# Mamba layer: the seven-tap convolution of the projected channels written as seven shifted projections

## The reference

```
zxbcdt = einsum('bld,ed->ble', u, W_in)          # u: normed x, 128 features
z, xBC, dt_raw = split(zxbcdt)                   # 256, 512 and 8 columns
xc = conv(transpose(xBC), conv_w, pad 3 and 3)   # 7 taps, each channel by itself
xBC = silu(transpose(xc + conv_b))               # x (256), and B and C of two directions
dt  = softplus(dt_raw + dt_bias)
...                                              # two scans over the tokens (forward, backward)
y = norm_w * (y / rms) * silu(z);  return y @ W_out
```

## Time and profile before

| | |
|---|---|
| median of 3 runs | 5271.6 us (5269.07 to 5281.68) |
| the profiled execution's own time | 5270.87 us |
| its span, first to last instruction | 5269.1 us |
| TensorE busy | 83% of the span |
| VectorE busy | 62% |
| ScalarE busy | 53% |
| GpSimd busy | 22% |
| mean granted TensorE clock | 0.87 of full |

### The profile page before, as it was taken

How to read it: one execution, slowest core, us unless ns; L and a number is a source line. 1 busy time by engine, 2 the same in 40 slices (tenths; PEclk the granted TensorE clock), 3 DMA queues, 4 the chain that set the end, 5 groups by cost and what they waited for, 6 DMA issues and landing times.

```text
span 5269.1 us, 95794 instructions
## 1 busy us (share of the span) xinstructions
PE 4377.1 (83%) x38234; PEld 1845.2 (35%) x38234; DVE 3290.1 (62%) x4913; ACT 2818.4 (53%) x5188; POOL 1137.6 (22%) x1318
## 2 busy tenths in 40 slices
PE   4888867888876657745699999999999999999995
PEld 2333433434444424423123333333222222333343
DVE  4778434344533564553797777676798999776831
ACT  2667533132222222230386667776789888666761
POOL 2221011011000222222123323242211112232413
PEclk7999988788887666565799999999999999999997
DMA  2222010000000000000211011101011111111000
GB/s 80 54 55 55 2 35 21 2 20 9 13 1 7 0 0 1 0 0 27 49 45 38 14 38 20 38 14 38 14 45 44 44 32 33 38 20 38 14 2 17
DMA packets 100288, 133.85 MB, mean 25 GB/s; under 512 B 48194, under 2 KB 60994, under 8 KB 99348
## 3 DMA queue, kind: packets, MB, share of 16 engines
q1 hardware_dynamic: 99860, 127.92, 9.9%
HBM read 63.50 MB, written 54.00 MB: 22 GB/s over the span
## 4 chain that ended last, share of the span: by engine, by line
PE 41%; DVE 8%; ACT 2%; issue 1%; POOL 1%; DMA 0%; SPq 0%; POOLq 0%; DVEq 0%; ACTq 0%
PE ps L1058 14%; PE ps L1031 8%; PE ps L1088 6%; DVE stream_max_pieces L1236 6%; PE ps L1043 5%; PE ps L1135 5%; PE ps L1077 1%; PE ps L1083 1%; ACT stream_probs L1153 1%; PE ps L1107 0%; PE ps L1120 0%; DVE stream_stats L1292 0%; DVE stream_stats L1273 0%; ACT L1153 0%; SPq L1471 0%
## 5 line engine op out<-in xcount | busy, mean ns | idle before, releaser
L1236 DVE TENSOR_REDUCE stream_max_pieces<-ps 128x2 f32<-128x1024 f32 x1536 | 1808.8, 1216 | 415.7 <-PE ps L1043 410.6
L1153 ACT ACTIVATE stream_probs<-ps 128x512 f32<-128x512 f32 x3072 | 1655.6, 597 | 486.5 <-PE ps L1031 468.0
L1058 PE MATMUL ps<-stream_probs,stream_v 128*16 128x256 f32 x12288 | 986.4, 394 | 20.6 <-issue 19.9
L1043 PE MATMUL ps<-stream_k_stack,stream_q_stack 48*128 48x512 bf16 x3072 | 645.3, 394 | 97.9 <-DVE stream_max_pieces L1236 64.6
L1031 PE MATMUL ps<-stream_q_stack,stream_k_stack 51*128 51x512 bf16 x3072 | 657.2, 394 | 13.7 <-ACT stream_probs L1153 9.3
L683 DVE TENSOR_REDUCE alibi_max_pieces<-ps 128x2 f32<-128x1024 f32 (+3 forms) x384 | 355.4, 952 | 140.6 <-PE ps L528 131.3
L1058 PEld LDWEIGHTS ps<-stream_probs,stream_v 128*16 128x16 f32 x12288 | 202.8, 94 | 654.1 <-issue 431.9
L624 ACT ACTIVATE alibi_probs<-ps 128x512 f32<-128x512 f32 (+3 forms) x768 | 333.9, 492 | 177.5 <-PE ps L509 142.9
L1031 PEld LDWEIGHTS ps<-stream_q_stack,stream_k_stack 51*128 51x128 bf16 x3072 | 173.1, 93 | 724.3 <-ACT stream_probs L1153 581.9
L308 POOL CAST stream_negmax_parts<-stream_negmax_t 128x32 bf16<-128x32 f32 x96 | 20.3, 212 | 1442.0 <-DVE stream_negmax_t L1225 1404.2
L1088 PE MATMUL ps<-stream_x1T,stream_w 128*128 128x512 f32 x512 | 282.6, 642 | 0.0
(11 more groups left out here) (412 smaller groups left out, 5752.0 us busy)
## 6 DMA issues: line engine op xcount, KB each, us to landing
stream_q_terms_dram<-stream_q_parts SPq DMA_DIRECT2D x72, 256.0 KB
stream_k_terms_dram<-stream_k_parts SPq DMA_DIRECT2D x72, 256.0 KB
stream_q_stack<-stream_q_terms_dram SPq DMA_DIRECT2D x96, 192.0 KB, 3.8
stream_k_stack<-stream_k_terms_dram SPq DMA_DIRECT2D x96, 192.0 KB, 4.4
delta_v_shifted<-delta_v_padded SPq DMA_DIRECT2D x64, 158.0 KB, 3.5
alibi_q_terms_dram<-alibi_q_parts SPq DMA_DIRECT2D x24, 256.0 KB
alibi_k_terms_dram<-alibi_k_parts SPq DMA_DIRECT2D x24, 256.0 KB
alibi_q_stack<-alibi_q_terms_dram SPq DMA_DIRECT2D x32, 192.0 KB
```

Source lines behind the costliest of these rows:

```text
L1043: ins = e.matmul(c.ps[:, mbank(key) + r, :], qs[R, buf, pair, qt * P:(qt + 1) * P], ks[R, buf, pair, kh * 512:kh * 512 + 512], start=True, ...
L1058: ins = e.matmul(c.ps[32 * j:32 * j + 16, 7, Q], v[:, b % 2, kt, GH * g + j, :], pr[:, (u + j // 2) % RP, j % 2, Q], start=(n == 0 and k = ...
L1153: e.activation(pr[:, u % RP, r, :], c.ps[:, ebank(key), :], ACT.Exp, scale=SCALE).then_inc(s_ed, 1)
L1236: e.tensor_reduce(mx[:, j % 2, kh, 4 * pair + qt % 4, :], c.ps[:, mbank(key):mbank(key) + 2, :], AXX, ALU.max).then_inc(s_md, 1)
```

## The change

The convolution and the projection are both linear along different axes, so the sum over taps can be taken over projections: for tap j the projection weights are scaled, column by column, by that tap, and are multiplied with `xT` shifted by j tokens; seven such products are accumulated in PSUM. `xT` gets three zero columns at either end, `pre` is gone, and `conv_out` too.

- `conv_rows` is a new input, 128 x 7 x 512 float32, 1792 KB: each row holds all taps of the 512 channels. It is loaded with the layer's weights.
- VectorE makes the scaled weights `wc` (`mamba_shifted_weights`) once, with seven products of 128x512, ahead of its first norm.
- TensorE does 56 matmuls of 512 columns per batch in place of 8.
- ScalarE applies bias and Silu straight from PSUM, in place of the copies into `pre`; the four Silus behind the first exponential are gone.
- VectorE's 28 operations per batch (lines 2475, 2478) are gone.

```diff
@@ -159,13 +159,13 @@
-    def __init__(self, core, name, ctx, banks, eps=1e-5):
-        self.c, self.banks, self.eps = core, banks, eps
+    def __init__(self, core, name, ctx, banks, eps=1e-5, pad=0):
+        self.c, self.banks, self.eps, self.pad = core, banks, eps, pad
         self.stats = core.sb(name + "_stats", [P, TPB, 6], F32, ctx)
...
         self.xn = core.sb(name + "_xn", [P, TPB, D], F32, ctx)
-        self.xT = core.sb(name + "_xT", [P, L], F32, ctx)
+        self.xT = core.sb(name + "_xT", [P, L + 2 * pad], F32, ctx)
         self.s_stats = core.sem(name + "_stats_done")
@@ -211,7 +211,7 @@
         for h in range(2):
-            e.activation(self.xT[:, h * 512:(h + 1) * 512], self.c.ps[:, self.banks[h], :], ACT.Copy).then_inc(self.s_xT, 1)
+            e.activation(self.xT[:, self.pad + h * 512:self.pad + (h + 1) * 512], self.c.ps[:, self.banks[h], :], ACT.Copy).then_inc(self.s_xT, 1)
@@ -2229,12 +2229,15 @@
     core.load(name, tri, "triangles")
+    rows = core.sb("conv_rows", [P, TAPS, 4 * P], F32)
+    core.load(name, rows, "conv_rows")
...
     with ExitStack() as ctx:
-        norm = Norm(core, name, ctx, (0, 1))
+        norm = Norm(core, name, ctx, (0, 1), pad=TAPS // 2)
+        xT = norm.xT[:, TAPS // 2:TAPS // 2 + L]
         sb = lambda n, shape, dt=F32: c.sb(f"{name}_{n}", shape, dt, ctx)
-        pre = sb("preconv", [P, 4, L + TAPS - 1])
+        wc = sb("shifted_weights", [P, TAPS, 4 * P])
         act = sb("conv_out", [P, 3, L])
@@ -2286,20 +2289,22 @@
             e.wait_ge(norm.s_xT, 2 * (b + 1))
-            for i in range(4):
-                if i >= 2:
-                    e.wait_ge(s_pjc, 4 * b + i - 1)
-                for k in range(2):
-                    m = e.matmul(bank(2 + 2 * (i % 2) + k), w[:, MW_X + i * P:MW_X + (i + 1) * P], norm.xT[:, k * 512:(k + 1) * 512], start=True, stop=True)
+            e.wait_ge(s_wc, TAPS)
+            for q, i in enumerate((3, 2, 0, 1)):
+                if q >= 2:
+                    e.wait_ge(s_act, 4 * b + q - 1)
+                for j in range(TAPS):
+                    for k in range(2):
+                        m = e.matmul(bank(2 + 2 * (q % 2) + k), wc[:, j, i * P:(i + 1) * P], norm.xT[:, k * 512 + j:k * 512 + j + 512], start=(j == 0), stop=(j == TAPS - 1))
                 m.then_inc(s_pj, 1)
             for t in range(NC_):
-                m = e.matmul(bank(0, 8 * t, 8), norm.xT[:, t * P:(t + 1) * P], w[:, MW_DT:MW_DT + 8], start=True, stop=True)
+                m = e.matmul(bank(0, 8 * t, 8), xT[:, t * P:(t + 1) * P], w[:, MW_DT:MW_DT + 8], start=True, stop=True)
             m.then_inc(s_dtr, 1)
...
                 for t in range(4):
-                    m = e.matmul(bank(6 + t // 2, (t % 2) * SI, SI), norm.xT[:, (4 * r + t) * P:(4 * r + t + 1) * P], w[:, MW_Z:MW_Z + SI], start=True, stop=True)
+                    m = e.matmul(bank(6 + t // 2, (t % 2) * SI, SI), xT[:, (4 * r + t) * P:(4 * r + t + 1) * P], w[:, MW_Z:MW_Z + SI], start=True, stop=True)
                 m.then_inc(s_z, 1)
@@ -2312,7 +2317,7 @@
                 if n < 2:
-                    e.wait_ge(s_pjc, 4 * b + 4)
+                    e.wait_ge(s_act, 4 * (b + 1))
                 else:
@@ -2391,9 +2396,10 @@
             norm.scalar(e, b)
-            for i in range(4):
-                e.wait_ge(s_pj, 4 * b + i + 1)
-                e.activation(pre[:, i, 3:3 + L], flat(2 + 2 * (i % 2)), ACT.Copy).then_inc(s_pjc, 1)
+            for q, i in enumerate((3, 2, 0, 1)):
+                e.wait_ge(s_pj, 4 * b + q + 1)
+                dst = cs[:, 1:1 + L] if i == 3 else act[:, i, :]
+                e.activation(dst, flat(2 + 2 * (q % 2)), ACT.Silu, bias=w[:, MW_CB + i:MW_CB + i + 1]).then_inc(s_act, 1)
             for r in range(2):
@@ -2408,12 +2414,6 @@
                 e.activation(ex[:, n % 2, :], bank(2 + n % 2), ACT.Exp).then_inc(s_ex, 1)
-                if n == 0:
-                    for q, i in enumerate((3, 2, 0, 1)):
-                        e.wait_ge(s_cv, TAPS * (4 * b + q + 1))
-                        alone(e, c)
-                        dst = cs[:, 1:1 + L] if i == 3 else act[:, i, :]
-                        e.activation(dst, conv_out[:, i, :], ACT.Silu).then_inc(s_act, 1)
             for g in range(6):
@@ -2434,13 +2434,13 @@
-    conv_out = mm[:, 0:8, :, :].rearrange("p (i a) h t -> p i (a h t)", i=4)
...
         e.wait_ge(s_w, n_w)
-        e.memset(pre[:, :, 0:3], 0.0).then_inc(s_pad, 1)
-        e.memset(pre[:, :, L + 3:L + 6], 0.0).then_inc(s_pad, 1)
+        e.memset(norm.xT[:, 0:3], 0.0).then_inc(s_pad, 1)
+        e.memset(norm.xT[:, L + 3:L + 6], 0.0).then_inc(s_pad, 1)
+        for j in range(TAPS):
+            e.tensor_tensor(wc[:, j, :], w[:, MW_X:MW_X + 4 * P], rows[:, j, :], ALU.mult).then_inc(s_wc, 1)
         e.memset(cs[:, 0:1], 0.0).then_inc(s_pad, 1)
@@ -2464,18 +2464,6 @@
-            for q, i in enumerate((3, 2, 0, 1)):
-                e.wait_ge(s_pjc, 4 * b + i + 1)
-                for j in range(TAPS):
-                    tap = w[:, MW_CONV + TAPS * i + j:MW_CONV + TAPS * i + j + 1]
-                    src = pre[:, i, j:j + L]
-                    if j == 0:
-                        alone(e, c)
-                        e.tensor_scalar(conv_out[:, i, :], src, tap, w[:, MW_CB + i:MW_CB + i + 1], ALU.mult, ALU.add).then_inc(s_cv, 1)
-                    else:
-                        e.wait_ge(s_cv, TAPS * (4 * b + q) + j)
-                        e.scalar_tensor_tensor(out=conv_out[:, i, :], in0=src, scalar=tap, in1=conv_out[:, i, :], op0=ALU.mult, op1=ALU.add).then_inc(s_cv, 1)
@@ -2593,6 +2581,8 @@
     cols += [np.broadcast_to(rows, (P, rows.size))]
+    taps = np.concatenate(tiles(conv[0:256], conv[256:512]), 0).T
+    r["conv_rows"] = np.ascontiguousarray(np.broadcast_to(taps[None], (P,) + taps.shape))
     r["w_mamba"] = np.ascontiguousarray(np.concatenate(cols, 1))
```

More of the change, by code:

```diff
@@ L2267, in mamba @@
     s_v, s_ms, s_pe, s_ri, s_yn, s_yT, s_yTc, s_o, s_x = S("vector_steps"), S("squares_summed"), S("eps3_added"), S("rms_inv_ready"), S("y_ready"), S("y_transposed"), S("yT_copied"), S("out_ready"), S("residual_ready")
-    s_zw = S("z_weighted")
+    s_zw, s_wc = S("z_weighted"), S("weights_shifted")
     NVS = 4 + 1
```

4 lines of the change are left out of this document (2 added, 2 removed).

## The result

The changed kernel takes 5285.3 us (median of 15 runs; the kernel before 5265.5 in its 15 runs, 6 us under the median of the three runs shown ahead). The ratio is 1.0042, with a 95% interval of 1.0026 to 1.0059: slower by 14 to 31 us. The prediction said 5301, 5284 to 5320, and +30.4 us.

The account below looks back on a forecast made before the run. The prediction took VectorE's convolution, for which TensorE waits 34.35 us per batch, as the bound. 164.8 - 137.4 - 0.7 - 3.7 + 4.4 + 3.0 = +30.4 us on 5270.9 gave 5301 us, range 5284 to 5320.

Parts of the forecast that it names:

- TensorE's added run: Projection: 96 more records per batch at 0.429 us each, hidden behind nothing, 41.2 us per batch, +164.8 us in all.
- rival of closer spacing: Folded projection: the long run's records lie closer than the short one's; 0.031 us less each takes 14 us; chance 0.02.
- rivals of 0.527: Folded projection: records spaced 0.527 us as in the alternating pairs, +44 us, 5345 us; chance 0.05.
- half clock in the run: Folded projection: TensorE at half clock in the run, 48 us more per batch, +192 us, 5493 us; chance 0.03.
- The wait removed: Decay loop's start: TensorE no longer waits for the convolution's last tile and its Silu, -137.4 us over four batches.
- GpSimd's first products: Ahead of the loop: GpSimd's first two products no longer slowed beside VectorE's convolution in two batches, -0.7 us.
- The clock in the loop: Decay loop's first 20 us: slow stretches 2.0 us shorter per batch, -3.7 us; bounds -15.3 and +0.9.
- Behind the loop: From the transposes to the residual, four batches: no change predicted, 0.
- Start of the layer: Once per run: waiting for 1792 KB more of loads, +4.4 us, and seven weight products ahead of the first norm, +3.0.
- The sum: All terms of the prediction together: +30.4 us on 5270.9, giving 5301 us.
- The rival "the clock does not fall": TensorE keeps full clock through the 4.77 us gap ahead of the sums: -22.8 us, 5279 us; chance 0.07.

Follow-up runs that it names:

- one_tap: The changed kernel with only the middle of the seven taps multiplied, the other six left out of the computation; ratio to the kernel before 0.9747, layer 631.9 us.
- wait_filled_37: The kernel before, with 37 matmuls whose result nobody reads put where TensorE waits for the Silus; ratio to the kernel before 0.9988, layer 753.6 us.
- half_each: The changed kernel with two tiles folded on TensorE, two convolved by VectorE, dt and z ahead of the folded matmuls; ratio to the kernel before 0.9812.
- gap_filled: The changed kernel with five unread matmuls of 512 columns in TensorE's gap ahead of the decay sums; ratio to the kernel before 1.0015, layer 774.8 us.
- bf16_folded: The changed kernel with bf16 operands in the folded products, dt and z left in float32; ratio to the kernel before 0.9753, layer 654.5 us.
- late_products: The changed kernel with conv_rows on its own semaphore and the seven weight products behind VectorE's first norm; timed once, 5281.6 us, layer 782.3 us.
- rates_first: The changed kernel with dt and half of z ahead of the folded matmuls, the rest of z between them; ratio to the kernel before 0.9965, layer 764.4 us.

## Why the prediction was right, and where it was not

**How close it was.** The layer's +24.4 on the base that the prediction used, 5270.9, would be 5295, inside the forecast's own 5288 to 5312. The measured 5285.3 is outside of that and only 1 us above the lower end of the wider 5284 to 5320. By the prediction's mark of 5287.4 for slower, worked out from three runs of the kernel before, 5285.3 alone would not be slower; it is against the 15 runs beside it, and by the layer.

**TensorE's added run** (+164.8): right, +164.6. The three things that the old projection did not show (accumulation, 48 us at a stretch, a new weight at each tap) cost nothing, and the shifted reads neither. The rival of closer spacing falls: 0.43 per record over 112 records, and the 0.213 of bf16 fits a price by the pass. So do the rivals of 0.527 and of half clock in the run.

**The wait removed** (-137.4) and GpSimd's first products (-0.7): right. No wait of L2329 for a Silu is left; sums to first loop product take 0.65 us less over the four batches.

**The clock in the loop** (-3.7): right in sign, wrong in size, and this is the step that failed. I wrote that the clock would rise as long after the loop's start as it did after the resumption. The piece from the sums to the transposes fell by 151.1 us; less 137.4 and 0.7 that leaves -13.0, near the lower bound of -15.3 that the text gave for four stretches as short as 4.4. By the same sum: 42.8 slow us before, 22.8 after, of which 8.0 are first products that were slow before too; 28.0 less x 0.46 = 12.9. one_tap shows that a short run with the same gap brings 46.8 slow us, so the length hangs on more than the loop itself, which my rule left out.

**Behind the loop** (0): +3.4. Windows of the stage from the transposes to the residual, second batch, in the kernel before and in the changed one:

```profile
1988.75:2087.65 98.90, 75.69 (x293) 0.57 0.00 0
```

```profile
2006.90:2107.40 100.50, 77.29 (x293) 0.56 0.00 1
```

Slow for 85 us and then for 88, with the same 293 records. wait_filled_37 has +6.4 in this stage. But a fast loop does not by itself cost it: half_each, whose four loops run at full clock, has 397.1 us here against the 398.1 of the kernel before, gap_filled 399.2 and bf16_folded 406.4. No edit touches the stage, and what sets its clock was not tried.

**Start of the layer** (+4.4 and +3.0): +4.6 and +2.9. late_products took both away, but for 1 us of the products.

**The sum** (+30.4): +24.4 in the layer. The 6.0 us between them are the clock's: 9.3 more gained in the loop, 3.4 lost behind it. The time itself came 16 us under the 5301 of the prediction: 6 of it are this, another 5.4 the base (5270.9 against 5265.5), and the rest, under 5 us, no run explains. That these errors went the same way and still stayed inside the range is luck.

**The rival "the clock does not fall"** (0.07) did not happen: the gap still cost the clock in all four batches. gap_filled shows what it would have been: 774.8 us of layer, +10.5 and not the +7.6 of its price.

**Shown and open.** Shown: the cost per pass, that the folded products are serial, that filling the gap ahead of the sums holds the clock and shortens the loop. Argued only: that the long run ahead of the gap is what shortens the slow stretches. Open: what makes a slow stretch 4 or 15 us long behind the same gap, and what sets the clock behind the loop.

## What to carry to other kernels

Moving work from one engine to another gains only what the two can then do at once; where the batch is serial, 34.4 us on VectorE for 41.2 on TensorE is a loss whatever the busy shares say, and half of the work on each engine, with the rates' inputs ahead, beat both versions by 2%. Before folding a filter into a float32 matmul, count passes: taps x 4 x 0.213 us per 512 columns here, and one pass in bf16. Look for the short gaps of TensorE ahead of a dense stage: either move the chain that causes it (the rates) ahead of the long run, or fill it. Begin a stage with wide matmuls and not with the narrowest. And judge such an edit on the layer's own time, with the stages behind it.

## What the runs showed of the hardware that I had not expected

- Behind the same gap of 4.77 us the slow stretch of the loop was 9.6, 4.4, 4.4 and 4.4 us after a dense run of 48 us, 12.0, 4.0, 6.8 and 6.8 after one of 12 us in bf16 (windows with clocks 0.70, 0.90, 0.83, 0.83), and 9.6, 15.2, 12.4 and 9.6 after one of 8 us. Between the first batches of the float32 kernels there is no difference.
- The gap's own length matters, but not by a sharp line: 1.02, 1.39 and 2.54 us cost nothing, 3.05 and 3.11 a stretch of over 12 us, while behind 1.46, 1.94 and 3.65 there was one of 3.6.
- What stands first in a batch can cost the clock. In the second to fourth batch of rates_first the clock was full at the first matmul and 0.50 under z, behind dt's 16 records of 8 columns; where records of 512 columns came first it stayed at 1.00. In the fourth batch dt and half of z took 2.30 and 3.76 us so, and 1.85 and 1.97 behind wide matmuls.
- 1792 KB more in flight did not delay the 866 KB issued ahead of them (released after 4.6 us, 4.9 without).
